# Group-norm attention layer: softmax sums on GpSimd in a batch's first four heads, turned by TensorE into the next scores' place

## What is computed

```python
h = group_norm(x, gn_w, gn_b)                       # 32 groups
q, k, v = (qkv_w @ h + qkv_b) as 8 heads of 64      # per batch
attn = softmax(q^T k / 8)                           # 1024 x 1024 a head
out = proj_w @ (v attn^T) + proj_b
x = x + out
```

## Time and profile before

| | us |
|---|---|
| median of 3 runs | 2790.56 (2786.41 to 2794.03) |
| profiled execution, its own time | 2791.04 |
| its span, first to last instruction | 2789.2 |
| PE busy | 2639.5 (95%) |
| DVE busy | 2103.8 (75%) |
| ACT busy | 1571.9 (56%) |
| POOL busy | 239.1 (9%) |

### The profile page before, as it was taken

How to read it: one execution, slowest core, us unless ns; L and a number is a source line. 1 busy time by engine, 2 the same in 40 slices (tenths; PEclk the granted TensorE clock), 3 DMA queues, 4 the chain that set the end, 5 groups by cost and what they waited for, 6 DMA issues and landing times.

```text
span 2789.2 us, 33182 instructions
## 1 busy us (share of the span) xinstructions
PE 2639.5 (95%) x11856; PEld 2192.5 (79%) x11856; DVE 2103.8 (75%) x3294; ACT 1571.9 (56%) x1930; POOL 239.1 (9%) x134
## 2 busy tenths in 40 slices
PE   6999999999999999999999999999999985989998
PEld 5788887888888888888888888888888764777776
DVE  6888768876887688778877887688768856788753
ACT  3767646764676467656765676467656732333321
POOL 1001001100100010000000000000000121000100
PEclk9999999999999999999999999999999997999999
DMA  4522241213122412231223132312122162655443
GB/s 159 170 58 76 57 125 47 80 54 125 47 79 58 125 46 81 61 118 46 84 58 118 46 88 54 118 51 83 54 87 88 53 238 103 227 198 181 172 153 143
DMA packets 154849, 279.48 MB, mean 100 GB/s; under 512 B 51776, under 2 KB 52032, under 8 KB 154176
## 3 DMA queue, kind: packets, MB, share of 16 engines
q1 hardware_dynamic: 152128, 268.98, 30.6%
q0 software_dynamic: 2560, 8.39, 0.9%
HBM read 180.04 MB, written 63.18 MB: 87 GB/s over the span
## 4 chain that ended last, share of the span: by engine, by line
PE 76%; DVE 15%; issue 4%; DMA 2%; ACT 1%; SPq 1%; POOL 0%; DVEq 0%; POOLq 0%; ACTq 0%
PE tiles L371 8%; PE tiles L372 8%; PE tiles L427 8%; PE tiles L373 8%; PE tiles L473 7%; PE tiles L450 7%; PE tiles L466 7%; PE tiles L467 7%; PE tiles L446 7%; DVE p_low L695 4%; PE tiles L1304 4%; DVE row_max L679 2%; PE tiles L1354 2%; DVE flags L1546 1%; DVE flags L1544 1%
## 5 line engine op out<-in xcount | busy, mean ns | idle before, releaser
L679 DVE TENSOR_REDUCE row_max<-tiles 128x1 f32<-128x512 f32 x1014 | 695.7, 687 | 412.5 <-PE tiles L427 407.9
L543 ACT ACTIVATE p_high<-tiles 128x1024 fp32r<-128x1024 f32 x512 | 525.8, 1027 | 616.2 <-PE tiles L450 615.5
L695 DVE TENSOR_TENSOR p_low<-p_full,p_high 128x1024 fp32r<-128x1024 f32 x512 | 667.8, 1304 | 6.0 <-ACT p_full L546 5.2
L546 ACT ACTIVATE p_full<-tiles 128x1024 f32<-128x1024 f32 x512 | 521.7, 1019 | 0.0
L427 PE MATMUL tiles<-k_high_low,q_high_high 128*128 128x512 f32 x1014 | 409.7, 404 | 7.5 <-DVE row_max L679 6.9
L466 PE MATMUL tiles<-p_high,v_high 128*128 128x512 f32 x1024 | 406.8, 397 | 2.1 <-ACT num_den L562 1.3
L467 PE MATMUL tiles<-p_high,v_low 128*128 128x512 f32 x1024 | 402.2, 393 | 0.0
L427 PEld LDWEIGHTS tiles<-k_high_low,q_high_high 128*128 128x128 f32 x1014 | 313.0, 309 | 63.6 <-DVE row_max L679 22.0
L473 PE MATMUL tiles<-p_low,v_high 128*128 128x512 f32 x1024 | 326.5, 400 | 15.5 <-DVE p_low L695 15.3
L878 POOL TENSOR_TENSOR o_normed<-num_den,o_normed 64x1024 f32<-64x1024 f32 x64 | 164.4, 2569 | 2050.1 <-DMA o_normed<-rec_rows 2050.1
L450 PE MATMUL tiles<-q_low_max,k_high_one 65*128 65x512 f32 x1024 | 325.6, 399 | 0.9 <-DMA q_low_max<-row_max_top 0.8
(11 more groups left out here) (167 smaller groups left out, 3169.9 us busy)
## 6 DMA issues: line engine op xcount, KB each, us to landing
x_tiles<-in_x SPq DMA_DIRECT2D x64, 512.0 KB, 4.8
w_high<-w_split SPq DMA_DIRECT2D x126, 256.0 KB, 2.8
w_low<-w_split SPq DMA_DIRECT2D x126, 256.0 KB, 2.9
k_high_one<-k_high_low SPq DMA_DIRECT2D x128, 128.0 KB, 2.3
q_high_high<-q_high_high SPq DMA_DIRECT2D x128, 128.0 KB, 2.3
o_normed<-rec_rows SPq DMA_DIRECT2D x64, 256.0 KB, 3.7
x<-x_tiles SPq DMA_DIRECT2D x32, 512.0 KB, 4.0
x_full<-x SPq DMA_DIRECT2D x32, 512.0 KB, 6.1
```

The source lines that it names most:

```text
L543: nc.scalar.activation(ph[:, r, :], ring[:, r, :], ACT.Exp, scale=ATT_SCALE).then_inc(s_ph, 1)
L679: nc.vector.reduce_max(mcol[:, h % 2, n, i:i + 1], max_bank(h, i, n)[:, :], AX_X).then_inc(s_mx, 1)
L695: tt(pl[:, r, :], p32[:, r, :], ph[:, r, :].bitcast(F32), ALU.subtract).then_inc(s_pl, 1)
```

## The change

In heads 0 to 3 of each batch (`SUMMED`) the denominators are no longer made by the ones beside v. v_low and v_high stand side by side in one block (`vs`), one matmul multiplies p_high by both, another p_low by both, and the two halves of `pv` are added: ScalarE copies one half to SBUF (`numer_denom`), VectorE adds the other (`numerators`). The sums of p over the keys are made in two parts. GpSimd adds up the four p_full tiles of a half head (`add_up`, three additions of 128 x 1024) and the two halves of the result (`add_tiles`, 128 x 512); TensorE turns the 128 x 512 sums by four transposes (`turn_sums`, a unit "d" in step 6 of the head for its first half and step 2 of the next head for its second) into the ring's buffer in which the next step's scores will stand; VectorE sums over the former partitions (`denominators`), straight into the columns that `reciprocal` reads. The next scores wait for that (s_dsum). `p_full` of step t now also waits until the addition that reads p_full(t-2) is done (s_sum); the first addition of a half reads two tiles.

In heads 4 to 7 the ones stay, in the new block; the matmul with v_low writes 64 rows only, and ScalarE makes a second copy, of the denominators' row.

The output units are spread over steps 9 to 24 from head 0 (heads 1 to 3), the second pair's units start later, `tile_stats` moves to steps 3, 5, 7 of head 3 and step 0 of head 4, the o_high and o_low of the first pair go to head 3, `reciprocal` to the start of step 3, the reciprocals' DMAs one step earlier, `normalise` waits for p_low of step 4, and the last store of x1 moves from head 2 to head 3.

```diff
+SUMMED = (0, 1, 2, 3)
+SUM_HEADS = [h for h in range(ALL_HEADS) if h % HEADS in SUMMED]
+ONE_HEADS = [h for h in range(ALL_HEADS) if h % HEADS not in SUMMED]
...
+def step_of_sum(u):
+    return u[1] * STEPS + (6 if u[2] == 0 else STEPS + 2)
...
 PAIR_STEPS = (begins(0, 1, 6, 8, 2, 3, 3, 5, whole=(("k", 0), ("k", 1), ("v", 0), ("q", 1))),
-              begins(1, 3, 5, 8, 10, 12, 12, 14),
+              begins(3, 4, 9, 10, 12, 13, 14, 15, whole=(("k", 0), ("q", 0), ("v", 0))),
...
+OUTPUT_STEPS = {(0, 0): (9, True), (0, 1): (10, False), (1, 0): (12, False), (1, 1): (14, False), (2, 0): (16, True),
+                (2, 1): (17, False), (3, 0): (22, True), (3, 1): (23, False)}
...
+    for h in SUM_HEADS:
+        for i in range(2):
+            t = step_of_sum(("d", h, i))
+            put(t // STEPS, t % STEPS, ("d", h, i))
...
         if kind == 0 and g > 0:
-            o = [("o", b0 - 1, t, i) for t in range(CT) for i in range(2)]
-            for s in range(7):
-                put(b, 1 + s, o[s])
-            put(a + 2, 0, o[7])
+            for (t, i), (s, whole) in OUTPUT_STEPS.items():
+                (put if whole else spread)(a + s // STEPS, s % STEPS, ("o", b0 - 1, t, i))
...
+STATS = [(3, 3), (3, 5), (3, 7), (4, 0)]
...
+                at += {"g": 1, "vt": 2, "d": 2}.get(u[0], 6 * len(parts))
+                if u[0] != "d":
+                    take(u)
+            at += 3 if is_summed(h * STEPS + s - 1) else 5
...
+    with nc.sbuf_tensor("den_rows", [P, 2, N], F32) as den_rows:
+        den = den_rows[96:97, :, :]
     q2 = sb("q_low_max", [P, 3, N], F32R)
-    v1 = sb("v_high", [P, 2, NT, 3, HD], F32R)
-    v2 = sb("v_low", [P, 2, NT, 3, HD], F32R)
+    vs = sb("v_parts", [P, 2, NT, 2, 3, HD], F32R)
...
-    nd = sb("num_den", [P, 2, N])
+    num = sb("numerators", [P, N])
+    psum = sb("p_sums", [P, N])
...
+        def turn_sums(u):
+            t = step_of_sum(u)
+            pe.wait_ge(s_sum, 4 * half_sum(*u[1:]) + 4)
+            pe.wait_ge(s_p32, t)
+            for j in range(4):
+                last = nc.tensor.transpose(ring[:, (t + 1) % 2, j * P:(j + 1) * P], psum[:, j:HALF:4], ident[:, :])
+            last.then_inc(s_unit, 1)
...
+            for u in UNITS.get(before(h, s), []):
+                if u[0] == "d":
+                    pe.wait_ge(s_dsum, half_sum(*u[1:]) + 1)
...
-        def weights_of(v, t, n):
+        def weights_of(kind, t, n):
             h, j = t // STEPS, 2 * (t % 4) + n
-            return v[:, (h // 2) % 2, j, h % 2:h % 2 + 2, :].rearrange("p a d -> p (a d)")
+            blocks = dict(both=slice(0, 2), ones=slice(1, 3), low=slice(0, 1))[kind]
+            return vs[:, (h // 2) % 2, j, h % 2, blocks, :].rearrange("p a d -> p (a d)")
...
-                pe.wait_ge(s_nd, t // 4)
+                if is_summed(t - 1):
+                    pe.wait_ge(s_num, sum_of(t - 1) + 1)
+                else:
+                    pe.wait_ge(s_den, ones_read(t - 1))
...
-                mm(pv[:, :], weights_of(v1, t, n), p, start=(t % 4 == 0 and n == 0), stop=False)
-                last = mm(pv[:, :], weights_of(v2, t, n), p, start=False, stop=False)
+                for kind in ("both",) if is_summed(t) else ("ones", "low"):
+                    last = mm(pv[0:HD if kind == "low" else P, :], weights_of(kind, t, n), p, start=(t % 4 == 0 and n == 0 and kind != "low"),
+                              stop=False)
             last.then_inc(s_phu, 1)
         def weigh_low(t):
             pe.wait_ge(s_pl, t + 1)
             for n in range(2):
-                last = mm(pv[:, :], weights_of(v1, t, n), pl[:, t % 2, n * HALF:(n + 1) * HALF],
-                          start=False, stop=(t % 4 == 3 and n == 1))
+                last = mm(pv[:, :], weights_of("both" if is_summed(t) else "ones", t, n),
+                          pl[:, t % 2, n * HALF:(n + 1) * HALF], start=False, stop=(t % 4 == 3 and n == 1))
...
+            if t > 1 and is_summed(t - 2):
+                act.wait_ge(s_sum, added(t - 2))
             nc.scalar.activation(p32[:, r, :], ring[:, r, :], ACT.Exp, scale=ATT_SCALE).then_inc(s_p32, 1)
...
+            mine, others = slice(a * HD, (a + 1) * HD), slice((1 - a) * HD, (2 - a) * HD)
             act.wait_ge(s_plu, t + 1)
             if i == 0 and h > 1:
                 act.wait_ge(s_on, h - 1)
-            nc.scalar.activation(nd[:, h % 2, i * HALF:(i + 1) * HALF], pv[:, :], ACT.Copy).then_inc(s_nd, 1)
+            nc.scalar.activation(num[mine, i * HALF:(i + 1) * HALF], pv[others if is_summed(t) else slice(0, HD), :],
+                                 ACT.Copy).then_inc(s_nd, 1)
+            if not is_summed(t):
+                if ones_up_to(h) > 1:
+                    act.wait_ge(s_dcol[a], 32 * (ones_up_to(h) - 1))
+                nc.scalar.activation(den[:, a, i * HALF:(i + 1) * HALF], pv[HD:HD + 1, :], ACT.Copy).then_inc(s_den, 1)
...
-            if h % 2 == 0 and h > 0 and s == 7:
+            if h % 2 == 0 and h > 0 and h % HEADS != 2 and s == 7:
                 o_high(h // 2 - 1)
+            if h % HEADS == 3 and s == 1:
+                o_high((h - 2) // 2)
...
+        def numerators(t):
+            h, i = t // STEPS, (t % STEPS) // 4
+            mine = slice(h % 2 * HD, (h % 2 + 1) * HD)
+            to = num[mine, i * HALF:(i + 1) * HALF]
+            dve.wait_ge(s_nd, t // 4 + 1)
+            tt(to, pv[mine, :], to, ALU.add).then_inc(s_num, 1)
+        def denominators(u):
+            a = u[1] % 2
+            dve.wait_ge(s_unit, unit(u))
+            if u[1] > 1:
+                dve.wait_ge(s_rec, u[1] - 1)
+            nc.vector.reduce_sum(dcol[:, a, 4 * u[2]:4 * u[2] + 4],
+                                 ring[:, (step_of_sum(u) + 1) % 2, 0:HALF].rearrange("p (j k) -> p j k", j=4), AX_X
+                                 ).then_inc(s_dsum, 1)
...
-            dve.wait_ge(s_dcol[a], 16 * (h // 2 + 1))
+            if h in SUM_HEADS:
+                dve.wait_ge(s_dsum, half_sum(h, 1) + 1)
+            else:
+                dve.wait_ge(s_dcol[a], 32 * ones_up_to(h))
             nc.vector.reciprocal(rcol[:, a, :], dcol[:, a, :]).then_inc(s_rec, 1)
...
+            if h > 0 and s == 3:
+                reciprocal(h - 1)
...
+                if t % 4 == 1 and t > 1 and is_summed(t - 2):
+                    numerators(t - 2)
                 p_low(t - 1)
             if block:
                 reduce_max(*block, 0)
+            for u in UNITS.get((h, s), []):
+                if u[0] == "d":
+                    denominators(u)
...
-                    tile_stats(b, (1, 3, 4, 5).index(s))
+                if (h % HEADS, s) in STATS:
+                    tile_stats(b, STATS.index((h % HEADS, s)))
...
-            if h % 2 == 1 and h > 1 and s == 0:
+            if h % 2 == 1 and h > 1 and h % HEADS != 3 and s == 0:
                 o_low(h // 2 - 1)
-            if h > 0 and s == 3:
-                reciprocal(h - 1)
+            if h % HEADS == 3 and s == 2:
+                o_low((h - 2) // 2)
...
+        def add_up(t):
+            first = t % 4 == 1
+            h, i = t // STEPS, t % STEPS // 4
+            pool.wait_ge(s_pl, t + 1)
+            if first:
+                pool.wait_ge(s_p32, t + 1)
+                pool.wait_ge(s_on, max(h - 1 + i, 0))
+                if sum_of(t) > 0:
+                    pool.wait_ge(s_unit, unit(("d", *SUM_HALVES[sum_of(t) - 1])))
+            else:
+                pool.wait_ge(s_sum, 4 * sum_of(t) + t % 4 - 1)
+            nc.gpsimd.tensor_tensor(psum[:, :], p32[:, (t - 1) % 2, :] if first else psum[:, :], p32[:, t % 2, :],
+                                    ALU.add).then_inc(s_sum, 1)
+        def add_tiles(h, i):
+            pool.wait_ge(s_pl, h * STEPS + 4 * i + 5)
+            pool.wait_ge(s_sum, 4 * half_sum(h, i) + 3)
+            nc.gpsimd.tensor_tensor(psum[:, 0:HALF], psum[:, 0:HALF], psum[:, HALF:N], ALU.add).then_inc(s_sum, 1)
...
+            if h + 1 in SUM_HEADS:
+                pool.wait_ge(s_sum, 4 * half_sum(h + 1, 0) + 4)
+            elif h in SUM_HEADS:
+                pool.wait_ge(s_sum, 4 * half_sum(h, 1) + 4)
             pool.wait_ge(s_nd, 2 * h + 2)
+            if h in SUM_HEADS:
+                pool.wait_ge(s_num, half_sum(h, 1) + 1)
             if a == 1:
                 pool.wait_ge(s_rstd, min((h + 3) // HEADS + 1, BATCH))
-            nc.gpsimd.tensor_tensor(on[rows, :], nd[rows, a, :], on[rows, :], ALU.mult).then_inc(s_on, 1)
...
-        for h in range(1, ALL_HEADS):
+        for h in range(ALL_HEADS):
             b = h // HEADS + 1
             if h % HEADS == 5 and b < BATCH:
                 rstd(b)
-            normalise(h - 1)
+            if h - 1 in SUM_HEADS:
+                add_up((h - 1) * STEPS + 7)
+                add_tiles(h - 1, 1)
+            if h in SUM_HEADS:
+                for s in range(1, 4):
+                    add_up(h * STEPS + s)
+                add_tiles(h, 0)
+            if h > 0:
```

(24 more changed lines are left out.)

47 lines of the change are left out of this document (29 added, 18 removed).

## The result

| | before | after |
|---|---|---|
| median, us | 2792.3 (2786.41 to 2795.78) | 2818.39 (2815.47 to 2820.95, 4 runs) |
| ratio, 95% interval | | 1.0095 (1.0074 to 1.0117) |
| profiled execution, us | 2791.04, span 2789.2 | 2819.89, span 2818.1 |
| PE / DVE / ACT / POOL busy, us | | 2601.6 / 2219.8 / 1612.2 / 782.9 |

The change makes the kernel 26 us slower (21 to 33 by the interval); the forecast was 14 us faster. The time lies inside the range, on the side of rival B, and mostly for another reason than B gives.

The account below looks back on a forecast made before the run. TensorE, by its number of matmuls, was taken as the bound, with VectorE next. The terms -118 + 51 + 29 + 27 + 2 + 3 - 8 = -14 us gave 2776 us, range 2712 to 2830 (own range 2755 to 2798).

Parts of the forecast that it names:

- rival B: Summed heads: the GpSimd/VectorE lock is the bound and slower, a head mean of 38 against 36.5 us; 2838 us; chance 0.25.
- Matmuls, -118: Summed heads, TensorE: two matmuls fewer a step, 512 at 0.23 us, all on the path; -118 us.
- Transposes, +51: TensorE, 64 halves of four transposes of the sums at 0.8 us; +51 us (22 to 53).
- The likeness to L427: Transposes' strided weight loads, priced like an existing load with that stride: 309 ns against 189, 0.12 us more each, nothing hidden.
- The chain through p_full, +29: Steps 6 and 7: p_full waits for GpSimd's addition, p_low follows late, TensorE waits 0.9 us a head; +29 us (0 to 70).
- -8: TensorE's wait of L371 for row_max and some of head 3's waits go with the moved units; -8 us.
- the two stall terms: TensorE's added waits: +29 us by the chain through p_full, +27 us by VectorE's added work.
- The lock: GpSimd and two-SBUF-input VectorE operations exclude each other: held 29.0 of 34 us a head, p_low's mean 1.6 to 2 us.
- VectorE, +27: Numerator additions and row sums, 2.7 us a summed head, make VectorE late around head 3: 3.4 us x 8, +27 us (0 to 45).
- Moves, 0: Output and second-pair units, weight loads, stores and the wait on s_den move to other steps; costed at nothing.
- A: The stalls hide in the slack, both stall terms fall away; 2720 us, or 2692 with cheap transposes; chance 0.25.
- C: Steps 2 and 6: next scores wait for late row sums, 64 x 0.8 = 51 us; 2771 or 2798 us; chance 0.08.

Follow-up runs that it names:

- experiment 1: The changed kernel with the first batch's four summed heads given the ones columns back; measured 2799.0 us, ratio 1.0021.
- e10: The changed kernel with p_full not waiting for GpSimd's operations, which read two other tiles at full length (2410 ns; sums wrong); 2772.6 us, ratio 0.9920.
- run 2: The changed kernel with no summed head (`SUMMED = ()`), so only the moved units and waits stay; 2798.78 us, ratio 1.0027.
- e3: The changed kernel with GpSimd's additions cut to 32 columns (253 ns each, sums wrong), p_full still waiting for them; 2751.5 us, ratio 0.9854.
- e7: The changed kernel with VectorE's numerator additions on 16 of 512 columns and row sums over 4 of 128 (results wrong); 2799.28 us, ratio 1.0027.
- Run 5: The changed kernel with VectorE's added work nearly taken out (numerators on 16 columns, row sums over 4 elements); 2799.28 us, 19 us less than the changed kernel.

## Why the prediction was wrong

**Batches are not alike: the step that failed most.** All terms were taken from one batch in the middle and multiplied by 32 heads or 8 batches. The sum says -1.8 us a batch. The six middle ones measured +0.4 each, the last +2.2, the first +20.5. That makes 22 of the 43 us between the forecast and the measured span; the middle six are 13, the last 4, the second layer 4. The first batch should have been costed by itself: its head 1 has no output units and had 26.16 us of TensorE work in 29.66, so "All of it lies on the path" was false there. The saved matmuls gave nothing, and the waits that the additions bring came on top. Rival B's condition, a summed head over 36.5 us because TensorE isn't ahead, holds in this place (40.5), and a part of B's cause too: the additions hold up VectorE's splitting of weights there (experiment 1).

**Matmuls, -118.** The count is right and 0.23 us a piece is right; it is the return that is missing.

**Transposes, +51.** Mis-sized. Four of them, and the matmul behind:

```profile
948.15 0.63 PE L459 MATMUL tiles<-identity,p_sums 128*128 128x128 f32 x4
948.54 0.47 PE L428 MATMUL tiles<-o_high,w_high 128*128 128x512 f32 x1
```

They move the next matmul by 0.39 us, here and as the median of the 64 places: 26 us in all, near the forecast's lower bound of 22. The strided weight load does take longer (205 ns beside 140 ns for the contiguous one of 128x128), but the transposes start 0.119 us apart beside 0.109: nearly all of it is hidden. The likeness to L427 was a likeness of duration, and durations of weight loads are no prices; the prediction says that of matmuls and didn't keep to it here.

**The chain through p_full, +29.** The mechanism is right, and so is where it was laid out by hand: 1.6 and 0.8 us in heads 0 and 1 were forecast, 1.71 and 1.45 measured (means of the six middle batches: how late the product with the p_low of step 6 starts, between steps 7 and 8); TensorE's idle time before products with p_low grew from 15.5 to 39.3 us in the whole. The 0.9 us of the mean leave 0.9 for head 3, for which nothing was laid out. What failed is "TensorE comes back for that p_low" as its only end. ScalarE's queue is served in order, so what stands behind the waiting p_full waits too. In head 3:

```profile
1020.46 2.38 POOL L1019 TENSOR_TENSOR o_normed<-numerators,o_normed 64x1024 f32<-64x1024 f32 x1 [0.22 <-issue]
1021.50 2.43 DVE L783 TENSOR_TENSOR p_low<-p_full,p_high 128x1024 fp32r<-128x1024 f32 x1
1024.01 2.37 POOL L998 TENSOR_TENSOR p_sums<-p_full 128x1024 f32<-128x1024 f32 x1 [1.17 <-DVE p_low L783]
...
1026.47 1.02 ACT L624 ACTIVATE p_full<-tiles 128x1024 f32<-128x1024 f32 x1 [4.53 <-POOL p_sums L998]
1027.39 0.68 ACT L670 ACTIVATE v_full<-tiles,columns 128x512 f32<-128x512 f32 x1
...
1028.22 0.63 PE L439 MATMUL tiles<-identity,v_full 128*128 128x128 f32 x4 [1.39 <-ACT v_full L670]
```

The normalising product holds up p_low, p_low the addition, the addition p_full. v_full has nothing to do with the sums, and the last projection matmul ahead of it had started at 1022.58, 3.9 us before ScalarE was free; TensorE loses 1.39 us to it once a batch. In e10, without the tie, this wait is gone. TensorE's waits of 400 to 2000 us, the answer to the earlier trace rows:

```profile
PE tiles L549 <- DVE p_low L783: 19.3, 22, 1.6
PE tiles L495 <- DVE row_max L767: 16.2, 33, 1.5
PE tiles L428 <- DVE row_max L767: 10.4, 15, 1.0
PE tiles L439 <- ACT v_full L670: 8.3, 6, 1.4
```

The first line was forecast, the other three are 35 us where before had 10.7, and where the sum had -8 for them in the whole layer. The waits for row_max (26.6 us here) come with the sums (11.9 in run 2), but neither with the tie (29.2 in e10) nor with the length (23.2 in e3) nor with VectorE's added work alone (24.3 in e7); what makes them isn't shown. Read from the distances of starts, TensorE's time beyond its usual spacing went from about 8 to about 18.5 us in a middle batch: +10 to +11, where the two stall terms made 7.0. A middle batch is then -14.7 of matmuls, +3.3 of transposes and +10.5 of stalls, about -1 together, and +0.4 was measured: the cheap transposes nearly paid for the dear stalls, so that the forecast for a middle batch was within 2.2 us by two errors of opposite sign, which is luck.

**The lock.** "p_low's mean 1.6 to 2 us" is wrong: 1297 ns, against 1304 before. The two do exclude each other, as the earlier trace rows showed, and after's trace has it again: the 128x4 operation takes 1.81 us beside an addition that ends with it.

```profile
951.02 2.40 POOL L998 TENSOR_TENSOR p_sums<-p_full 128x1024 f32<-128x1024 f32 x1 [0.23 <-POOL o_normed L1019]
...
951.63 1.81 DVE L775 TENSOR_TENSOR row_max_top<-row_max 128x4 fp32r<-128x4 f32 x1
```

(The lock as the Trainium skill gives it, "SBUF — State Buffer", the section on two separate sides, stands: whoever starts first has it for the whole instruction.) But an addition waits for the p_low of its own step and starts right behind it, and mostly is done before the next. I had added up holders of the lock as if each meeting were left to chance. Meetings there are all the same, and the mean hides them: 40 of the 512 p_low took over 1.5 us (26 before), 32 of them beside an addition (step 7 of heads 0 to 2 and step 3 of head 1, once in nearly every batch) and 7 beside the normalising product in step 5 of head 3. Those at step 7 cost TensorE no wait, which is the slack that the prediction gave them; the p_low of 2.43 us in head 3 above, beside the normalising product, stands in the chain. The normalising product's tie to p_low, costed at nothing, took many of its old meetings away: in run 2 p_low's mean is 1258 ns.

**VectorE, +27.** Run 5 says 19. **Moves, 0.** Run 2 says 7 (4 to 11): head 4 and the queue order at the layer's end. The sentence that failed is that on what stands behind the wait on s_den.

**The signs named beforehand.** TensorE's waits for p_low are over 20 us in the whole, so not A; heads 0 to 2 of the middle batches (36.4, 36.4, 36.8) stand at B's limit of 36.5, though mostly by the tie and not by B's lock (35.2, 34.9 and 35.5 in e10, which keeps the lock); the scores waited for row sums 0.8 us in all, so not C. GpSimd is 783 us busy, where "near 600" was wrong even by the prediction's own 19.2 us a head.

## What to carry to other kernels

When a new reader is put on a double buffer, ask what stands ahead of that reader in its own queue, and what stands behind the writer in its queue; here folding into two accumulators in turn, with each piece read at once, cost 2.5 us more GpSimd time a head and gave back 55 us. Cost the first and the last round of a loop by themselves: an engine that is the bound in the middle may have time at the edges, where a saving gives nothing, and another engine may have work only there (here the splitting of weights). An entry with a wait, moved ahead of a large transfer in a DMA queue, delays that transfer too, here into a small one that TensorE waited for.
